# A three-stage decoder on one core: the products of cross attention in wide GpSimd instructions, and gathers that read the slot table directly

## The reference, cut to what matters

```
Q, K, V = (x @ Wq.T + bq), (c @ Wk.T + bk), (c @ Wv.T + bv)      # each to (rows, 16 heads, 16 channels)
score  = einsum('bshd,bsgd->bshg', Q, K)
weight = softmax(score, axis=-1)
attn   = einsum('bshg,bsgd->bshd', weight, V)
out    = attn @ Wo.T + bo
```

## Time and profile before

| what | us |
| --- | --- |
| median of 3 runs (lowest, highest) | 3036.44 (3029.61, 3038.48) |
| profiled execution, its own time | 3033.89 |
| its span in the profile | 3032.2 |
| POOL, L1804 (products with values), 512 instructions, busy | 369.5 |
| POOL, L1797 (products with keys), 512 instructions, busy | 358.9 |
| PE busy, share of the span | 2750.8 (91%) |
| DVE busy, share of the span | 2487.2 (82%) |
| POOL busy, share of the span | 2111.9 (70%) |

### The profile page before, as it was taken

The page is one execution under the profiler, slowest core; times in us unless marked ns, Lnnn a source line. Parts: engine busy times, 40 slices in busy tenths (PEclk is TensorE's granted clock), DMA queues, the critical chain, the costliest instruction groups (busy, mean ns, idle before and its releaser), DMA issues. The chain is left out here.

```text
span 3032.2 us, 68140 instructions
## 1 busy us (share of the span) xinstructions
PE 2750.8 (91%) x22096; PEld 2295.9 (76%) x22128; DVE 2487.2 (82%) x5452; ACT 1954.2 (64%) x4120; POOL 2111.9 (70%) x2651
## 2 busy tenths in 40 slices
PE   6999999999999999999788499667999999999978
PEld 3888888888888888888555299535777777777767
DVE  6888888888888888888599577468899898989863
ACT  5888878778787877878444155346666666666642
POOL 5897666666666666666468544369888989898870
PEclk9999999999999999999899699768999999999989
DMA  4555444444444444444444399600000000000000
GB/s 144 172 193 169 133 143 139 144 135 146 137 131 153 131 143 132 155 131 128 142 152 146 134 337 333 207 15 18 20 19 27 21 25 24 22 24 22 21 5 11
DMA packets 185881, 340.09 MB, mean 112 GB/s; under 512 B 40668, under 2 KB 104037, under 8 KB 178936
## 3 DMA queue, kind: packets, MB, share of 16 engines
q1 hardware_dynamic: 179448, 319.55, 32.6%
q0 software_dynamic: 6144, 16.79, 1.8%
HBM read 264.68 MB, written 63.19 MB: 108 GB/s over the span
## 5 line engine op out<-in xcount | busy, mean ns | idle before, releaser
L1804 POOL TENSOR_TENSOR l_prod<-l_sco,l_kv 128x256 f32<-128x256 f32 x512 | 369.5, 760 | 36.4 <-DVE l_sco L2311 36.4
L1797 POOL TENSOR_TENSOR l_prod<-l_q,l_kv 128x256 f32<-128x256 f32 x512 | 358.9, 743 | 47.3 <-DVE l_att L2319 47.3
L718 DVE SCALAR_TENSOR_TENSOR a_cq<-a_PQ,a_taps,a_cq 128x504 f32<-128x504 f32 (+2 forms) x384 | 281.7, 734 | 72.7 <-ACT a_cq L584 63.6
L718 DVE SCALAR_TENSOR_TENSOR a_ck<-a_PK,a_taps,a_ck 128x504 f32<-128x504 f32 (+2 forms) x384 | 280.6, 731 | 9.7 <-ACT a_ck L584 0.5
L342 POOL TENSOR_TENSOR a_tq<-a_cq,a_tq 128x512 f32<-128x512 f32 x128 | 165.9, 1296 | 131.2 <-ACT a_tq L590 131.1
L329 POOL TENSOR_TENSOR a_hrs<-a_hve,a_neghalf 128x8 f32<-128x8 f32 x128 | 209.6, 1638 | 25.7 <-DVE a_hve L735 25.2
L485 PE MATMUL a_Y<-a_wo,a_og_parts 128*128 128x256 f32 x1536 | 205.9, 284 | 5.0 <-POOL a_og_parts L336 5.0
L412 PEld LDWEIGHTS a_X<-a_wv,a_xb 128*128 128x128 f32 x1536 | 200.0, 188 | 12.1 <-issue 1.2
L342 POOL TENSOR_TENSOR a_tk<-a_ck,a_tk 128x512 f32<-128x512 f32 x128 | 163.6, 1278 | 62.8 <-ACT a_tk L590 62.8
L412 PE MATMUL a_PQ<-a_x_hi,a_wqk 128*128 (+1 forms) x512 | 194.1, 420 | 12.6 <-issue 11.9
L412 PE MATMUL a_X<-a_wv,a_xb 128*128 128x256 f32 x1536 | 204.2, 282 | 0.8 <-DMA a_xb<-a_x_lo 0.8
(11 more groups left out here) (398 smaller groups left out, 8380.6 us busy)
## 6 DMA issues: line engine op xcount, KB each, us to landing
a_wqk<-qk_parts SPq DMA_DIRECT2D x112, 512.0 KB, 3.4
m_wgu<-gate_up_parts SPq DMA_DIRECT2D x39, 1024.0 KB, 8.1
a_wv<-v_parts SPq DMA_DIRECT2D x56, 512.0 KB, 3.8
a_wg<-g_parts SPq DMA_DIRECT2D x112, 256.0 KB, 3.3
a_wo<-o_parts SPq DMA_DIRECT2D x112, 256.0 KB, 2.9
a_dr<-decays SPq DMA_DIRECT2D x256, 64.0 KB, 2.6
m_hs<-sorted_rows SPq DMA_DIRECT2D x39, 256.0 KB, 7.1
sorted_outs<-m_ys SPq DMA_DIRECT2D x39, 256.0 KB, 7.5
```

Of the source, the lines that this page charges most:

```text
L718: nc.vector.scalar_tensor_tensor(out=acc, in0=src, scalar=taps[p][:, tap + k:tap + k + 1], in1=acc, op0=ALU.mult, op1=ALU.add).then_inc(s_ ...
L1797: nc.gpsimd.tensor_tensor(out=prod[:, h], in0=qv[:, h:h + 1, :].to_broadcast([P, H, HD]), in1=kk, op=ALU.mult).then_inc(S("E_pqk"), 1)
L1804: nc.gpsimd.tensor_tensor(out=prod[:, h], in0=sco[:, h:h + 1, :].to_broadcast([P, HD, H]), in1=vv, op=ALU.mult).then_inc(S("E_pav"), 1)
```

## The change

The 16 instructions of `products_qk` become four of four heads each, 128 x 1024 elements; queries are repeated over the key heads and keys over the four query heads by access patterns of stride 0. `products_av` is changed in the same way. The semaphores `E_pqk` and `E_pav` now count four a tile instead of 16, and every wait on them is rewritten: DVE still waits for a group of four heads before it sums it, SP for all products with values before it loads `kv` again. `gather` loses the copy and the two fence operations, and its DMAs take their row numbers from `slots` directly.

```diff
-        of_tile, ready = sb("of_tile", [P, 2], mybir.dt.uint32), sb("ready", [P, 1])
...
-                    sp.wait_ge(S("E_pav"), H * (t - 2))
+                    sp.wait_ge(S("E_pav"), 4 * (t - 2))
...
-                for h in range(H):
-                    nc.gpsimd.tensor_tensor(out=prod[:, h], in0=qv[:, h:h + 1, :].to_broadcast([P, H, HD]), in1=kk,
-                                            op=ALU.mult).then_inc(S("E_pqk"), 1)
+                for k in range(4):
+                    heads = slice(4 * k, 4 * k + 4)
+                    nc.gpsimd.tensor_tensor(out=prod[:, heads], in0=qv[:, heads, :].unsqueeze(2).to_broadcast([P, 4, H, HD]),
+                                            in1=kk.unsqueeze(1).to_broadcast([P, 4, H, HD]), op=ALU.mult).then_inc(S("E_pqk"), 1)
...
-                for h in range(H):
-                    nc.gpsimd.tensor_tensor(out=prod[:, h], in0=sco[:, h:h + 1, :].to_broadcast([P, HD, H]), in1=vv,
-                                            op=ALU.mult).then_inc(S("E_pav"), 1)
+                for k in range(4):
+                    heads = slice(4 * k, 4 * k + 4)
+                    nc.gpsimd.tensor_tensor(out=prod[:, heads], in0=sco[:, heads, :].unsqueeze(2).to_broadcast([P, 4, HD, H]),
+                                            in1=vv.unsqueeze(1).to_broadcast([P, 4, HD, H]), op=ALU.mult).then_inc(S("E_pav"), 1)
...
             def gather(t):
-                wait_if(pool, S("G_ready"), 2 * t)
                 wait_if(pool, S("G_x"), 2 * t)
-                nc.gpsimd.tensor_tensor(out=ready[:], in0=neghalf[:, 0:1], in1=neghalf[:, 0:1], op=ALU.mult).then_inc(S("G_ready"), 1)
-                nc.gpsimd.tensor_copy(of_tile[:], slots[:, tile(t), :].rearrange("p t k -> p (t k)")).then_inc(S("G_at"), 1)
-                pool.wait_ge(S("G_ready"), 2 * t + 1)
-                pool.wait_ge(S("G_at"), t + 1)
-                nc.gpsimd.tensor_tensor(out=ready[:], in0=neghalf[:, 0:1], in1=neghalf[:, 0:1], op=ALU.mult).then_inc(S("G_ready"), 1)
                 for k in range(2):
                     nc.gpsimd.indirect_dma_start(got[k][:], None, outs[:, :],
-                                                 bass.IndirectOffsetOnAxis(ap=of_tile[:, k:k + 1], axis=0)).then_inc(S(f"G_in{k}"), 16)
+                                                 bass.IndirectOffsetOnAxis(ap=slots[:, t, k:k + 1], axis=0)).then_inc(S(f"G_in{k}"), 16)
...
             def e_q(t):
-                wait_if(act, S("E_pqk"), H * t)
+                wait_if(act, S("E_pqk"), 4 * t)
...
                 def piece(t):
-                    wait_if(dve, S("E_pav"), H * t)
-                    dve.wait_ge(S("E_pqk"), H * t + 4 * k + 4)
+                    wait_if(dve, S("E_pav"), 4 * t)
+                    dve.wait_ge(S("E_pqk"), 4 * t + k + 1)
...
-                    dve.wait_ge(S("E_pav"), H * t + 4 * k + 4)
+                    dve.wait_ge(S("E_pav"), 4 * t + k + 1)
```

## The result

| | us |
| --- | --- |
| before, median of 4 runs (lowest, highest) | 3037.46 (3029.61, 3044.65) |
| after, median of 4 runs (lowest, highest) | 3119.54 (3114.14, 3121.59) |
| ratio, 95% interval | 1.0268 (1.0245 to 1.0290) |
| forecast, range | 3098, 3034 to 3112 |

The kernel became slower, as forecast, but by 82 us instead of the 65 of the sum; the measured time lies 7.5 us above the range. The profiled execution of after has a span of 3118.3 us, against 3032.2.

A forecast was written before the change was run, and what follows sets the result against it. It took the loop from `oD` through PE and `et_x` back to `oD`, 30.0 us a tile, as the bound, with DVE's list nearly as long. Sum: 3033.9 + 67 + 6 - 8 = 3098 us; range 3034 to 3112.

The forecast's parts named there:

- The price of a wide product: POOL's 128x1024 product: forecast 2.3 us, between 2.18 us and no gain at 2.77 us.
- The gather at nothing: POOL's gather loses at most 1.1 us a tile, but other waits cover it, so it was costed at nothing.
- The wait as the rest of the running product: DVE's two-SBUF-operand instructions wait out POOL's running product: `combine` 2.7 us more, `ft_gm_lo` 1.8 us more, `f_x2lo` none.
- The base tile: DVE's tile with all stages running: 28.4 + 2.7 + 1.8 = 32.9 us, against 30.0 us before.
- The front and the rest of the kernel: Outside the 23 tiles: 6 us more in the five iterations before, half of 16.8 us of DVE's waits saved.
- as that is more than 30.0 it sets the pace; PE gets slack: In the 23 tiles, DVE's 32.9 us replaces the 30.0 us loop, costing 23 x 2.9 = 67 us.
- The forecast's own list of signs: Expected in the profile after: DVE's wait before `et_x` gone, PE's wait for `oD` longer, tiles of 32 to 33 us.
- Only `combine` waits: Rival: `ft_gm_lo` slips in between products, so DVE's tile is 30.7 to 31.2 us, say 3054 us; chance 0.20.
- Faster: Rival: DVE's waits stay as they are and only waits for products go, 3017 us at best; chance 0.10.
- nothing: Rival: same mechanism with less to gain, or `combine` alone losing about DVE's 1.6 us slack, 3025 to 3043; chance 0.14.
- Much slower by lost boundaries: Rival: DVE misses the next product boundary; `combine` waiting for the batch's end gives 35.8 us tiles, 3167 us; chance 0.06.
- the one `f_x2lo` of the earlier trace: One DVE `f_x2lo` took 2.84 us beside products of 0.69 us, so it passed several boundaries; cited for much slower.

The follow-up runs named there:

- e3: The changed kernel with all products narrow again, leaving only the gather change: 3031.9 us, 0.9990 of before.
- e5: The changed kernel with `ft_gm` writing its product to PSUM, so `ft_gm_lo` reads only one operand from SBUF: 3095.9 us, 1.0206 of before.
- e2: The changed kernel with the products with keys narrow again, those with values still wide: 3101.7 us, 1.0220 of before.
- e4: The changed kernel with eight 128x128 matmuls done twice in PE's `f_qk`, result unchanged: 3103.4 us, 1.0241 of before.
- e10: The changed kernel with products of two heads (128x512, eight a batch) instead of four: 3038.9 us, 1.0013 of before.
- e6: e5 with `combine` moved in DVE's list to where POOL has no batch: 3059.0 us, 1.0079 of before.
- e1: The changed kernel with the products with values narrow again, those with keys still wide: 3028.2 us, 0.9995 of before.

## Why the prediction was wrong in its size

**Right.** The price of a wide product (2.40 and 2.46 us from the groups, forecast 2.3, inside the bounds of 2.18 and 2.77). The gather at nothing (e3). The wait as the rest of the running product, in its three places: `combine`, `ft_gm_lo`, and none for `f_x2lo`. The base tile: 32.9 to 33.1 us measured, 32.9 forecast. That POOL's shorter batches are worth nothing while DVE arrives after POOL. The front and the rest of the kernel sum to -0.8 us against the forecast's -2, and `split_low` met wide products (10.6 us for its three instructions instead of 6.7).

The Trainium skill, SBUF — State Buffer, section Who interferes with whom, states that a DVE instruction with two SBUF inputs contends with GpSimd's reads and one with at most one SBUF input, outside the modes that use two ports, does not. The runs agree on both sides: 2.46 us against 0.28 us for `ft_gm_lo` beside the same wide products (after and e5).

**Wrong.** The step that failed is "as that is more than 30.0 it sets the pace; PE gets slack". It took PE's loop as a fixed 30.0 us and DVE's list as the longer of two. But PE waits for results of DVE in several places of a tile, and two of these, `oF` and `d_x`, lie behind `combine` in DVE's list. So the wait of `combine` lengthens PE's loop too, to 31.95 us (e2 and e5, where DVE still waits for it in nearly every tile), and only some 1 us of slack was left to PE. That by itself would not have cost anything, since DVE's 33.0 us were longer still. What it did cost is the second thing that the forecast left out: after such waits PE's clock fell, time and again, to 1.2 GHz for some microseconds. With that little slack PE then lasts longer than DVE: 31.95 us and 1.6 or 3.2 us for the fall are the tiles of 33.5 and 35.1 us. By an estimate from the same numbers, a loop of 30.0 us would have hidden nearly all of this, so both steps were needed for the miss.

Its size: 23 x (33.83 - 32.9) = 21 us, the distance from 3098 to the measured 3119.5 (the terms of the sum add up to 3098.9). Tile by tile it is 8 x 0.6 + 7 x 2.2 = 20 us. e4 tests it, since it keeps the products, the ports and DVE's order as they are: with PE's clock at 0.98, and no fall behind the wait for `d_x`, the tile is 32.93 us and the time 3103 us, 5 us from the forecast. The forecast's own list of signs had the wait for `oD` longer (24.4 instead of 17.2 us), but not that two others would join it.

The range was too narrow at its upper end for the same reason. It took in lost boundaries and a dearer product, both of which lie in DVE, and nothing that PE could lose.

**Rivals.** Only `combine` waits: e2 shows what that is, 3102 instead of the 3054 that I gave it, wrong by the same step. Faster, and nothing: no. Much slower by lost boundaries: no row of `combine` or `ft_gm_lo` in the stage shows one; nothing here explains the one `f_x2lo` of the earlier trace rows.

**Open.** Why PE's clock falls in some tiles and not in others. Short tiles of after have the same waits for `x_sb` (0.98 us in the long tile and in the one behind it) with the clock at 1.00. e10 and e6 also wait in every tile, and e10's clock is 1.00 throughout. The Trainium skill, TensorE: Matmul & The Clock Gate, section A second HAM failure mode: psum-queue depth-cycling, tells of a kernel in which short idle times of PE between groups of matmuls make its clock fall and rise; the falls here, too, come behind short waits of PE, and the amount of waiting that it takes was not measured.

## What to carry to other kernels

Before widening GpSimd instructions to save their fixed cost, list the DVE instructions with two SBUF operands that run beside them: each can wait for the rest of one wide instruction, and taking one such operand from PSUM removes the wait. When a delay is put into one engine's list, follow every result behind it to the other engines before calling their time slack; a loop that two engines share has no fixed length. And when PE begins to wait where it did not, look at the granted clock of the work behind the wait: here its falls cost 21 us.

## What the hardware showed that was not expected

Eight more matmuls in every tile made the changed kernel 16 us faster, because PE's granted clock then fell less often (0.95 to 0.98 in the stage), and fell ahead of a wait that took the loss up. And the same wait of `ft_gm_lo`, 1.9 us, cost nothing by itself (e1) and 24 us over the kernel beside the wait of `combine` (after against e5).
